# Graph attention and expert kernel on one core: destination terms by head, an attention end that starts in pieces, later weights, and a reordered vector chain

## The reference, cut to what matters

```python
h = (x @ W).reshape(num_nodes, H, F)              # H = 4 heads, F = 64
al_s = einsum('nhf,hf->nh', h, a_s)
al_d = einsum('nhf,hf->nh', h, a_d)
e = leaky_relu(al_s[src] + al_d[dst], 0.2)
emax = segment_max(e, dst)
ee = exp(e - emax[dst])
alpha = ee / (segment_sum(ee, dst)[dst] + 1e-16)
out = segment_sum(alpha[:, :, None] * h[src], dst)
return out.reshape(num_nodes, H * F) + b
```

```python
shared = gelu(x @ W1s + b1s) @ W2s + b2s
h = gelu(einsum('bsd,edf->bsef', x, W1p) + b1p)   # 8 experts, hidden 1024
priv = einsum('bsef,efd->bsed', h, W2p) + b2p
```

## Time and profile before

| what | us |
|---|---|
| median of three runs | 6542.59 |
| lowest and highest of them | 6542.52, 15764.01 |
| the profiled execution's own time | 6540.51 |
| its span, first to last instruction | 6538.9 |
| DVE busy in the span | 3314.1 (51%) |
| PE busy | 4292.3 (66%) |
| POOL busy | 3662.1 (56%) |

### The profile page before, as it was taken

One profiled execution on the slowest core, in us unless ns is written; L12 is line 12 of the kernel. 1 busy time (PEld: TensorE's weight loads), 2 busy tenths in 40 slices (PEclk: granted clock), 3 DMA queues, 4 the chain that ended last, 5 costly groups with the idle time before them and its releaser, 6 DMA issues. The chain is left out here.

```text
span 6538.9 us, 91130 instructions
## 1 busy us (share of the span) xinstructions
PE 4292.3 (66%) x16953; PEld 3195.3 (49%) x16954; DVE 3314.1 (51%) x7793; ACT 826.7 (13%) x2019; POOL 3662.1 (56%) x3758
## 2 busy tenths in 40 slices
PE   1455667644656665455667369999992556666879
PEld 1333444433434443333444258888882444444745
DVE  7355666665566666566666731111114444444655
ACT  0200000020000002000000123322220000000322
POOL 3577777657777764777777047222222777775000
PEclk9777778876778887677888569999996777888889
DMA  5443333334333333433333233133334333333011
GB/s 174 123 113 106 106 106 106 89 110 120 106 106 106 106 95 99 124 106 106 106 106 100 84 123 88 37 66 58 60 51 117 105 105 105 105 105 96 23 49 43
DMA packets 495005, 627.74 MB, mean 96 GB/s; under 512 B 260172, under 2 KB 376904, under 8 KB 493256
## 3 DMA queue, kind: packets, MB, share of 16 engines
q0 software_dynamic: 191568, 486.53, 27.8%
q1 hardware_dynamic: 293816, 132.89, 7.6%
q10 hardware_dynamic: 9552, 7.61, 0.4%
HBM read 531.35 MB, written 95.78 MB: 96 GB/s over the span
## 5 line engine op out<-in xcount | busy, mean ns | idle before, releaser
L956 POOL DMA_INDIRECT rows<-table,ix x2352 | 2259.3, 961 | 741.2 <-issue 682.6
L1217 PE MATMUL acc<-rows,hot 128*128 x5856 | 1621.5, 435 | 228.0 <-DVE hot L1064 174.6
L1217 PEld LDWEIGHTS acc<-rows,hot 128*128 128x128 f32 x5856 | 1164.5, 211 | 641.4 <-issue 425.2
L1263 POOL DMA_INDIRECT rows<-emb,ix x784 | 742.0, 946 | 320.7 <-issue 229.0
L1064 DVE TENSOR_TENSOR hot<-lanes,drel 128x256 f32<-128x256 f32 x1464 | 610.2, 422 | 572.2 <-PE acc L1217 569.6
L1385 PE MATMUL acc<-rows,hot 128*128 x1952 | 582.6, 461 | 321.4 <-DVE hot L1306 308.0
L1058 DVE TENSOR_TENSOR rows<-rows,pw 128x1024 f32<-128x1024 f32 x588 | 711.6, 1210 | 0.0
L1385 PEld LDWEIGHTS acc<-rows,hot 128*128 128x128 f32 x1952 | 430.9, 232 | 456.4 <-issue 381.2
L1955 PE MATMUL p<-xt,w 128*128 128x256 f32 x2496 | 554.4, 380 | 25.4 <-DVE xt L2011 25.4
L1966 PE MATMUL p<-w,xT 128*128 128x256 f32 x2496 | 551.4, 379 | 0.0
L1955 PEld LDWEIGHTS p<-xt,w 128*128 128x128 f32 x2496 | 476.2, 191 | 90.7 <-issue 25.5
(11 more groups left out here) (405 smaller groups left out, 4372.9 us busy)
## 6 DMA issues: line engine op xcount, KB each, us to landing
rows<-table,ix POOLq DMA_INDIRECT x2352, 2.8
xg<-slots_in SPq DMA_DIRECT2D x632, 32.0 KB
table<-hs SPq DMA_DIRECT2D x147, 130.0 KB, 2.0
own_row<-table SPq DMA_DIRECT2D x21, 896.0 KB, 11.2
slots_in<-zsp SPq DMA_DIRECT2D x9, 1664.0 KB
xin<-in_x POOLq DMA_DIRECT2D x14, 896.0 KB, 5.7
rows<-emb,ix POOLq DMA_INDIRECT x784, 2.7
w<-in_W1all POOLq DMA_DIRECT2D x9, 1024.0 KB, 7.4
```

The lines of the kernel that those rows point to most:

```text
L956: pool.indirect_dma_start(rows[:, h * GB + k, 0:RW], None, table, bass.IndirectOffsetOnAxis(ap=ix[:, h, k:k + 1], axis=0)).then_inc(landed ...
L1217: ins = nc.tensor.matmul(A, hot[j][:, k, :], four[:, j * 2 + k, :], start=False, stop=False, skip_group_check=True)
L1263: pool.indirect_dma_start(rows[:, h * GB + k, 0:D], None, table, bass.IndirectOffsetOnAxis(ap=ix[:, h, k:k + 1], axis=0)).then_inc(landed[ ...
```

## The change

Four things are done.

- **Front.** Each head's scan announces itself, SP stores each head as soon as its scan is done (four DMAs in place of one), and each head's `dT` load waits only for its own store. SP issues the four stores first and the loads behind them.
- **Chain order.** In each group `shut`, `x`, `up`, `top` come ahead of `differ`; `scale_sums` moves behind `fore` and `back`; the first `hots` of a group moves ahead of the wait for `paid`.
- **Attention end.** The first block of seven tiles is worked in pieces of 1, 2 and 4 tiles; the other six blocks stay whole.
- **Weights.** The first routed expert's weights are asked for after the 98 scatters.

```diff
@@ attention_pass, SP
                 sp.dma_start(own, c.spread.rearrange("(p j) c -> p j c", p=P)).then_inc(re_read, 16)
-                sp.wait_ge(filled, 1)
-                sp.dma_start(c.d_rows[:, 0:EP].rearrange("h (p j) -> p h j", p=P), node).then_inc(wrote, 16)
-                sp.wait_ge(wrote, 16)
                 for h in range(H):
+                    sp.wait_ge(filled, h + 1)
+                    sp.dma_start(c.d_rows[h, 0:EP].rearrange("(p j) -> p j", p=P), node[:, h, :]).then_inc(wrote[h], 16)
+                for h in range(H):
+                    sp.wait_ge(wrote[h], 16)
                     sp.dma_start(c.dT[h * GB:(h + 1) * GB, :, :],
                                  c.d_rows[h, :].rearrange("(m b q) -> b m q", b=GB, q=P)).then_inc(got, 16)
@@ attention_pass, DVE, each group
-                        dve.wait_ge(kept, m + low + 2)
-                        differ(before)
                         linked(v.tensor_copy(shut[:, :], flat(c.penT[:, 1, ds(m), :])))
...
-                        dve.wait_ge(scaled, m + 1)
-                        scale_sums(before)
+                        dve.wait_ge(kept, m + low + 2)
+                        differ(before)
                         dve.wait_ge(rowed, m + 1)
...
+                        dve.wait_ge(scaled, m + 1)
+                        scale_sums(before)
                         scale_old()
...
                         v.tensor_copy(old[:, :], flat(accs[:, ds(low), :])).then_inc(saved, 1)
+                        hots(m * GP + low)
                         dve.wait_ge(paid, m + 1)
...
                             if l:
                                 weigh(h, l)
-                            hots(m * GP + low + l)
+                                hots(m * GP + low + l)
@@ attention_end, DVE
-                for i in range(NB):
-                    o = i * 3 + links
-                    tiles = slice(i * UT, (i + 1) * UT)
+                pieces = [(0, 1), (1, 3), (3, UT)] + [(i * UT, (i + 1) * UT) for i in range(1, NB)]
+                for piece, (low, high) in enumerate(pieces):
+                    i = low // UT
+                    o = piece * 3 + links
+                    tiles = slice(low, high)
...
-                    for k in range(UT):
-                        t = slice(i * UT + k, i * UT + k + 1)
+                    for n in range(low, high):
+                        k, t = n % UT, slice(n, n + 1)
@@ experts_gelu, POOL
                 load_weights(pool, slice(0, 1), 0)
-                load_weights(pool, slice(1, 2), 1)
                 for t in range(NT):
                     for j in range(2):
                         pool.indirect_dma_start(slots_in, ...)
+                load_weights(pool, slice(1, 2), 1)
                 pool.wait_ge(emptied, 1)
```

More of the change, by code:

```diff
@@ L909, in attention_pass @@
         link = sem("link")
-        re_read, filled, wrote, got = sem("re_read"), sem("filled"), sem("wrote"), sem("got")
+        re_read, filled, got = sem("re_read"), sem("filled"), sem("got")
+        wrote = [sem(f"wrote{h}") for h in range(H)]
         at_end, rows_in, rows_out, brought = sem("at_end"), sem("rows_in"), sem("rows_out"), sem("brought")
@@ L1009, in _ @@
                 for h in range(H):
-                    ins = v.tensor_tensor_scan(node[:, h, :], c.goes_on[:, :], own[:, :, h], node_carry[:, h:h + 1],
-                                               ALU.mult, ALU.add)
-                ins.then_inc(filled, 1)
+                    v.tensor_tensor_scan(node[:, h, :], c.goes_on[:, :], own[:, :, h], node_carry[:, h:h + 1],
+                                         ALU.mult, ALU.add).then_inc(filled, 1)
                 dve.wait_ge(got, 16 * H)
@@ L1451, in _ @@
                 links = ch.n
-                for i in range(NB):
-                    o = i * 3 + links
-                    tiles = slice(i * UT, (i + 1) * UT)
+                pieces = [(0, 1), (1, 3), (3, UT)] + [(i * UT, (i + 1) * UT) for i in range(1, NB)]
[3 more added lines that the diff above has]
+                    tiles = slice(low, high)
                     by_head = lambda ap: ap.rearrange("p t (h f) -> p t h f", h=H)
-                    wide = lambda ap: ap.rearrange("p t (h e) -> p t h e", e=1).to_broadcast([P, UT, H, HD])
+                    wide = lambda ap: ap.rearrange("p t (h e) -> p t h e", e=1).to_broadcast([P, high - low, H, HD])
                     sums = accs[:, tiles, 0:D]
@@ L1465, in _ @@
                     dve.wait_ge(own, o + 3)
-                    for k in range(UT):
-                        t = slice(i * UT + k, i * UT + k + 1)
+                    for n in range(low, high):
+                        k, t = n % UT, slice(n, n + 1)
                         bias = c.gbias[:, :].rearrange("p (o d) -> p o d", o=1)
                         if project:
-                            dve.wait_ge(turned, i * UT + (k + 1))
+                            dve.wait_ge(turned, n + 1)
                             v.tensor_tensor(fin[:, k:k + 1, :], accs[:, t, 0:D], bias, ALU.add).then_inc(fin_made, 1)
```

## The result

The changed kernel takes 6528.8 us (median of 18 runs, 6524.0 to 6534.0), the kernel before in the same session 6541.1: a ratio of 0.9976 with a 95% interval of 0.9964 to 0.9987. The forecast was 6527, its range 6510 to 6545. Two of the eighteen runs of the kernel before were far off (6616.0 and 15764.0 us) and hardly move its median. The profiled execution fell by 12.5 us, from a span of 6538.9 to 6526.4.

The account below looks back on a forecast made before the run. POOL's gathers were taken to pace groups 1 to 23, DVE and PE the later ones. Front 0, chain -6.3, ends -4.8 + 1.0, weights -5.0 made -15.1: 6525.4, as a median 6527 us, range 6510 to 6545.

Parts of the forecast that it names:

- The front: Start of each pass: four head-by-head stores let first loads go some 6 us earlier, off the path; value 0.
- rival A: The front was on the path: 6 us more per pass, 6509; sign, a pass shorter by over 4 us; chance 0.08.
- The weights: Before the experts: later weights free the software queue, so DVE's first rows come sooner; -5.0 us, ends -3 and -7.
- The chain: Six late group chains in each of three passes: x earlier, part given back, net 0.35 us each; -6.3 us.
- (c): Late chains: the first one-hots now precede the copy of `pw`, so PE starts 0.15 us later per chain.
- The pass: Gathers of each pass: POOL never stops, 1.26 us a gather, and sets the pace of groups 1 to 23.
- Rival B: The chain becomes longer: x gains little as PE's transpose comes late, 0.88 us given back, 6547.5 us; chance 0.17.
- The attention ends: Ends of layers 0 and 1: pieces start POOL's scatters 3.1 us sooner, 2.4 kept per layer; -4.8 us.
- 28.4 scatters in 52 us at 1.83: Attention end: POOL's scatters beside DVE's big operations at 1.83 us each; the other 20.6 follow at 1.28.
- Rival C: Contention eats the starts: POOL's head start all spent beside DVE, weights only -3; -8.3 us, 6534; chance 0.20.
- Layer 2: End of layer 2: DVE alone sets the end, and six more operations cost 1.0 us; +1.0.

## Why the prediction was right, and where it was not

That the total came within 2 us of the forecast is luck in part. Of its terms the chains came 4.1 us short, the ends 6.9 and layer 2 0.3, while the weights brought 1.0 more, the gathers 6.2 that nobody had forecast, and the unchanged start 1.4.

*The front, 0*: right. The chain of the first group began 4.3 us sooner (some 6 forecast) and POOL did not, alone or in the whole. The prediction's own sign for rival A, a pass shorter by over 4 us, did come in the second pass (4.5), but there the gathers (2.4) and the tail (2.1) made it, not the front.

*The weights, -5.0*: right and a little small, -6.0 in the change and -6.6 alone, by the wait that was named.

*The chain, -6.3*: the size was right by two errors. That `x` starts earlier and that `fore` and `carry` give part of it back came as worked out (0.65 and 0.26 us earlier in the last group, 0.6 and 0.2 forecast): with `x` alone first 0.53 net a chain against 0.52. The step that failed is (c), the masks, priced at 0.15 and measured at 0.45: in the last group it was 0.38 (9.60 against 9.22), since the pair began 0.12 later than the sum had it and PE began 0.27 behind the end of `weigh` where it had followed the mask by 0.17; and that group stood for all six, in one of which (the 24th of the first pass, 10.38 against 9.64) it was 0.74. So a late chain of the changed kernel is 0.12 us shorter (9.41 against 9.54) and not 0.35, and eighteen of them are the 2.2 us by which 172.5 behind the gathers became 170.3. What the order did bring lies in "*The pass*", where 1.26 us a gather was taken as POOL's own. The shift of the merge sum lets gathers pass it: those that began inside it took 10.0 us more than their 0.945 each in the three passes before and 3.4 in the changed kernel, and the gathers' stretch is 6.2 shorter; in the trace of the chain alone it is some 15 shorter than in its neighbours. Rival B fell (nothing became slower), though `x`'s gain was mostly given back, by the masks and not, as B had it, by a late transpose of PE.

*The attention ends, -4.8*: wrong, +2.1, which is within what the ends vary by from kernel to kernel. The first step was right, POOL's start 3.1 sooner by the sum and 3.46 by the trace. The failed step is "28.4 scatters in 52 us at 1.83": the mean of the earlier trace rows was taken as the price of a scatter beside DVE, but it is a mixture of waits for the ends of DVE's operations. In step with them POOL makes four scatters in a block of 8.5 us, and five in one of 9.1 where DVE waits for PE; starting sooner leaves the step as it is and only adds blocks of the first kind (five scatters of 2.63 us in the changed kernel's first end, one before). Rival C had this as "all spent beside DVE", and for this term it was right. Its price for the weights fell.

*Layer 2, +1.0*: right, 1.3.

The Trainium skill, SBUF - State Buffer, "Who interferes with whom", says that a VectorE instruction with at most one SBUF input, outside the 2-port modes that copies can enter, stays clear of GpSimd, while one with two SBUF inputs contends with an instruction that reads SBUF. The runs agree: 180 gathers at 0.946 us beside products with a PSUM operand, 19 at 1.150 beside the SBUF sum, and 49 at 0.945 once that sum reads PSUM; whether `old<-accs`, which held gathers with one input, ran in such a mode no run shows. They disagree with the inference, which the prediction quotes, that descriptor generation is left alone.

What stays open: the masks alone cost 17.5 us, and the traces place 14.2 of it behind the last gathers: 8.1 in the eighteen late chains, 1.8 in PE's transposes, which follow `terms` later, 1.7 in the products behind the chains and 2.7 in a later group 23. Another 2.9 stand in the two attention ends, which the edit does not touch and which take 209.7 to 213.8 us in the kernels without pieces. In the same way `x` first brought 9.6 in the chains but 15.9 behind the last gathers. Why the ends vary, and where in each pass the scans meet gathers (it differs from trace to trace), is not explained.

## What to carry to other kernels

A mean duration beside another engine may be a wait in disguise: before a head start is priced with it, line up the ends of both engines' instructions, and see whether one goes in step with the other. Where POOL's indirect transfers are the pace, give each large VectorE operation beside them one operand in PSUM, or cut it into short ones. Here the first was worth 18 to 20 us and the second some 5; with half of the change's new order and its other three parts they took 6545 us to 6486. And time the two halves of a reordering apart: here one was worth -20 us and the other +17, and together they looked like a small success (-10).

## What was not expected of the hardware

An indirect transfer of POOL that begins inside a VectorE operation with all its operands in SBUF, more than some 0.05 us after its start, ends 0.75 to 0.86 us after that operation ends (0.75 behind the scans, 0.83 behind the merge sum, 0.86 for scatters behind the long operations), so that 0.98 us becomes 1.75 or 2.63, and 0.95 once 3.75. And collisions repeat: because the chain's start hangs on the landing of a group's last gather, the same gather, the 8th of the next group, met the same sum at the same distance (0.09 to 0.10 us ahead) in 15 of the 28 groups of the first pass of the kernel before, so that moving one operation against the landing changed the pace of a whole pass: in the changed kernel only six gathers of the first pass are held by this sum.
